# The row maximum of the global attention: one VectorE instruction over four PSUM banks in place of four and a fifth over their results

## What is computed

```python
qh = _split_heads(jnp.einsum('bnq,qi->bni', x, Wq))        # 8 heads x 4096 tokens x 128
kh = _split_heads(jnp.einsum('bmc,ci->bmi', context, Wk))  # 8 heads x 1920 contexts x 128
vh = _split_heads(jnp.einsum('bmc,ci->bmi', context, Wv))
sim = jnp.einsum('hid,hjd->hij', qh, kh) * SCALE
mean = jnp.mean(sim, axis=-1, keepdims=True)
sim = (sim - mean) * ATTN_MATRIX_SCALE + mean
attn = jax.nn.softmax(sim, axis=-1)
out = jnp.einsum('hij,hjd->hid', attn, vh)
```

## Time and profile before

| | us |
|---|---|
| median of 3 runs | 4903.08 (4897.85 to 4910.84) |
| the profiled execution, its own time | 4901.11 |
| its span, first to last instruction | 4899.0 |
| TensorE busy | 4206.9 (86%) |
| VectorE busy | 3463.0 (71%) |
| ScalarE busy | 2265.4 (46%) |
| GpSimd busy | 518.2 (11%) |
| mean granted clock of TensorE, as a share of 2.4 GHz | 0.917 |

### The profile page before, as it was taken

The page is one execution under the profiler, slowest core; times in us unless marked ns, Lnnn a source line. Parts: engine busy times, 40 slices in busy tenths (PEclk is TensorE's granted clock), DMA queues, the critical chain, the costliest instruction groups (busy, mean ns, idle before and its releaser), DMA issues. The chain is left out here.

```text
span 4899.0 us, 72375 instructions
## 1 busy us (share of the span) xinstructions
PE 4206.9 (86%) x23248; PEld 3247.5 (66%) x23248; DVE 3463.0 (71%) x8155; ACT 2265.4 (46%) x5353; POOL 518.2 (11%) x953
## 2 busy tenths in 40 slices
PE   8989979996999999999999999998226888788686
PEld 6867767774787777787777777776014555555554
DVE  7976667666677777777777777777647777777445
ACT  3546645553565655555555655554311222222322
POOL 2320010104000000000000000000301112211300
PEclk9989989997999999999999999998557888888699
DMA  3000000000000000000000000000020000000101
GB/s 85 0 35 0 0 1 0 0 0 17 2 2 4 2 4 1 3 4 2 4 2 4 2 4 1 3 1 4 11 58 5 0 0 0 0 0 1 38 0 34
DMA packets 33807, 41.24 MB, mean 8 GB/s; under 512 B 5180, under 2 KB 30019, under 8 KB 33479
## 3 DMA queue, kind: packets, MB, share of 16 engines
q1 hardware_dynamic: 33544, 38.08, 2.7%
HBM read 33.61 MB, written 4.19 MB: 8 GB/s over the span
## 5 line engine op out<-in xcount | busy, mean ns | idle before, releaser
L1683 ACT ACTIVATE global_prob_t_high<-psum 128x512 fp32r<-128x512 f32 x960 | 569.9, 601 | 588.8 <-PE psum L1797 588.8
L1591 DVE TENSOR_TENSOR global_prob_t_low<-psum,global_prob_t_high 128x512 fp32r<-128x512 f32 x960 | 656.9, 690 | 252.4 <-ACT global_prob_t_high L1683 238.2
L1597 DVE TENSOR_REDUCE global_top<-psum 128x1 f32<-128x480 f32 x1024 | 666.3, 657 | 108.8 <-PE psum L1757 103.7
L1704 ACT ACTIVATE global_prob<-psum,global_bias 128x480 f32<-128x480 f32 x1024 | 674.3, 662 | 17.9 <-DVE global_bias L1600 15.1
L1797 PE MATMUL psum<-ident,global_prob 128*128 128x128 f32 x3840 | 568.4, 273 | 39.1 <-DVE global_prob_t_low L1591 38.0
L1797 PEld LDWEIGHTS psum<-ident,global_prob 128*128 128x128 f32 x3840 | 467.5, 141 | 197.8 <-DVE global_prob_t_low L1591 70.6
L1755 PE MATMUL psum<-global_prob_t_high,global_v_low 128*128 128x512 f32 x960 | 456.1, 475 | 1.0
L1755 PE MATMUL psum<-global_k_high,global_q_low 128*128 128x480 f32 x1024 | 390.7, 382 | 15.1 <-ACT global_prob L1704 12.7
L1757 PE MATMUL psum<-global_k_high,global_q_high 128*128 128x480 f32 x1024 | 392.0, 383 | 0.0
L1756 PE MATMUL psum<-global_k_low,global_q_high 128*128 128x480 f32 x1024 | 388.7, 380 | 0.0
L1756 PE MATMUL psum<-global_prob_t_low,global_v_high 128*128 128x512 f32 x960 | 379.6, 395 | 0.0
(11 more groups left out here) (445 smaller groups left out, 8091.4 us busy)
## 6 DMA issues: line engine op xcount, KB each, us to landing
x_res<-in_x SPq DMA_DIRECT2D x8, 512.0 KB, 9.7
moe_we<-in_expert_t SPq DMA_DIRECT2D x8, 512.0 KB, 7.7
out<-x_res SPq DMA_DIRECT2D x4, 1024.0 KB, 8.4
cho_wqkv<-in_L_ffn_Wqkv SPq DMA_DIRECT2D x2, 1536.0 KB
self_ctx_t<-in_ctx_t SPq DMA_DIRECT2D x2, 1440.0 KB, 12.9
sel_w<-in_L_xattn_W SPq DMA_DIRECT2D x2, 1024.0 KB, 11.9
global_ctx_t<-in_ctx_t SPq DMA_DIRECT2D x1, 1440.0 KB
sel_ctx_t<-in_ctx_t SPq DMA_DIRECT2D x1, 1440.0 KB
```

The costliest lines, as they stand in the source:

```text
L1591: dve.tensor_tensor(dst, psum, high.bitcast(F32), ALU.subtract).then_inc(ready.sem, 1)
L1597: ins = dve.tensor_reduce(top[:, c:c + 1], w.psum[:, c, 0:chunk], AX.X, ALU.max)
L1683: act.activation(dst, psum, ACT.Copy).then_inc(ready.sem, 1)
L1704: act.activation(prob[:, par, j, c * chunk:(c + 1) * chunk], w.psum[:, c, 0:chunk], ACT.Exp, bias=bias[:, j % 2:j % 2 + 1], scale=scale, a ...
```

## The change

`maximum` waits once, for the last of the four chunks, and takes the maximum over the two free dimensions of all four banks in one instruction, straight into `bias`. The tile `top` goes. The multiplication by -scale stays.

```diff
-    top = sb("top", [P, chunks])
...
             def maximum(n, j):

-                for c in range(chunks):
-                    dve.wait_ge(scores_psum.sem, scores_psum.count((n * QT + j) * chunks + c))
-                    ins = dve.tensor_reduce(top[:, c:c + 1], w.psum[:, c, 0:chunk], AX.X, ALU.max)
-                chain.link(ins)
-                chain.link(dve.tensor_reduce(bias[:, j % 2:j % 2 + 1], top[:, :], AX.X, ALU.max))
+                dve.wait_ge(scores_psum.sem, scores_psum.count((n * QT + j) * chunks + chunks - 1))
+                chain.link(dve.tensor_reduce(bias[:, j % 2:j % 2 + 1], w.psum[:, 0:chunks, 0:chunk], AX.XY, ALU.max))
                 dve.tensor_scalar(bias[:, j % 2:j % 2 + 1], bias[:, j % 2:j % 2 + 1], -scale, None,
                                   ALU.mult).then_inc(bias_ready.sem, 1)
```

## The result

The changed kernel takes **5135.93 us** (median of 4 runs, 5132.42 to 5145.42), the kernel before 4905.91 us beside it (4 runs, 4897.85 to 4910.84). The ratio is 1.0474, with an interval of 1.0452 to 1.0495: 4.7% slower. The forecast was 5172 us, 36 us too much; 5135.93 lies inside the range from 5095 to 5215.

A forecast was written before the change was run, and what follows sets the result against it. TensorE was taken as the bound of the changed stage. The profiled 4901 us plus 208 us of delays, mostly waits for low parts, plus 63 us of slow clock gave 5172 us, with a range from 5095 to 5215 us.

The forecast's parts named there:

- What bounds the kernel: In the changed stage TensorE is busy 2119.63 of 2175.00 us, so a saving on VectorE is worth nothing by itself.
- The price of the reduction: One reduction over four banks takes 2.16 us; the multiplication begins 2.24 us behind the last product, 1.32 us later than before.
- Who pays: TensorE waits for late low parts: 1.32 us in tiles 0 and 3, 1.0 in tile 1, 0.04 in tile 2.
- The change of heads: In the 7 quads that change heads, 1.3 us at tile 0, values hide most of the rest: 7 x 1.5 = 10 us.
- some 0.2 us at the end: At the end of a quad that changes heads, the part not hidden by the values, where the exponentials are waited for.
- Ahead of the loop: The first maximum loses 1.3 us, the next three gain 0.4 us each: nothing in sum.
- The clock: Behind 7 in 10 of tile 0's 1.9 us idle stretches, 56 in all, the clock falls, losing 1.6 us each: 63 us.
- Rival 1: The clock holds throughout, leaving only the delays: 4901 + 208 = 5109 us, span 5095 to 5125; chance 0.25.
- the case with the falls: The main forecast, delays plus a falling clock: 5172 us, span 5140 to 5215; chance 0.60.
- Rival 2: VectorE catches up late low parts in its pauses, so only tile 0 pays: 84 us, 4985 us; chance 0.06.
- Rival 3: Faster: where VectorE reaches the maximum after the last product, one instruction beats five; 97 us less, 4804 us; chance 0.03.
- Rivals 4 and 5: 4: slow clock lasts longer or also follows tile 3, above 5215 us, chance 0.04; 5: unseen cover, no difference, chance 0.02.

The follow-up runs named there:

- e1: The kernel before, with its four reductions and the small one, but all waiting for the last product: 5250.36 us, ratio 1.0707.
- e8: The kernel before with the one merged reduction in row tile 0 alone, four reductions in the other tiles: 5002.96 us, ratio 1.0193.
- e12: The kernel before with the one merged reduction in row tile 3 alone, four reductions in the other tiles: 4981.62 us, ratio 1.0148.
- e3: The kernel before with the one merged reduction in row tile 2 alone, four reductions in the other tiles: 4904.57 us, ratio 1.0001.
- e10: The changed kernel with TensorE's loop over the heads written out, so that it has no jump back: 5120.97 us, ratio 1.0425 to the kernel before.
- e6: The changed kernel with `sums` moved on VectorE from behind tile 0's maximum to behind the low part of k = 3: 5084.18 us, ratio 1.0362 to the kernel before.
- e2: The kernel before with an unneeded reduction on VectorE behind each multiplication by -scale, delaying the low parts but not ScalarE: 5075.05 us, ratio 1.0349.
- e7: The changed kernel with four unneeded products on TensorE behind tile 0's `output`, filling part of its wait: 5120.97 us, ratio 1.0435 to the kernel before.
- e9: e5 with TensorE's loop over the heads written out, the other engines keeping their loops: 4879.1 us, ratio 0.9939 to the kernel before.
- e11: e5 with the loops over the heads written out on TensorE, VectorE and ScalarE: 4866.56 us, ratio 0.9915 to the kernel before.
- e5: The kernel before with `sums` moved on VectorE from behind tile 0's maximum to behind the low part of k = 3: 4875.37 us, ratio 0.9939.

## Why the prediction was right, and where its sizes were off

**What bounds the kernel: right.** TensorE was the bound, and 173 us less of VectorE's work were worth nothing. The sign and the mechanism are shown by e1, in which the late start alone, without the new instruction, costs more than the change.

**The price of the reduction: right.** 2.16 us taken, 2158 ns measured; 2.24 us behind the last product, 2.23 measured.

**Who pays: right, tile by tile.** A plain interval was to grow by 3.68 us and grew by 3.46. Tile 0 was put at 1.32 us (1.3 in e8), tile 3 at 1.32 (1.2 in e12), tile 1 at 1.0 (0.9 to 1.0), tile 2 at 0.04 (nothing in e3). The error of 0.2 us is mostly tile 3, and makes 9 us over 40 intervals. The waits for low parts were to rise to about 240 us and rose to 211.2.

**The change of heads: too low.** The step was "some 0.2 us at the end" with "7 x 1.5 = 10 us". By intervals (tiles 1 to 3 of that quad and tile 0 of the next, 0.2 + 1.3 + 1.32 = 2.8 us) that forecast is 20 us for the seven; measured are 34, of which some 26 are delay and 8 falls. I had let the values hide the late low part of k = 14. They do hide TensorE's wait for it, but the start of the next head is not hidden: it follows that low part by about 4 us, with five gaps longer by 1.0 to 1.6 us, and behind four of them the clock fell. e10 shows it: without TensorE's jump the five gaps are gone, and the kernel is 15 us faster.

**Ahead of the loop: too low.** The forecast was "nothing in sum"; measured are 3.0 us up to the first `sums`, of which 1.3 are tile 0 of the first quad, forecast elsewhere, and 1.7 are left. The first maximum lost the 1.3 us. The second and the fourth gained 0.39 us each, but at the third VectorE was not late, as the forecast had it: it waited 1.45 us for the last chunk (reduction at 1249.43), and nothing was gained there.

All delays together were forecast at 208 us and measured at 210.

**The clock: the step that failed.** It was "I take it that the clock falls behind 7 in 10 of these stretches". The idle stretch came out as forecast, 1.87 us for 1.9, and each fall cost what was forecast, 1.58 us for 1.6. But only 11 of some 53 stretches in tile 0 were followed by one. That is 18 us in place of 63, and with the falls at the changes of heads 25. Against the profiled run, 5132.42 us, the forecast was 40 us too high: 38 us of it are the clock and 4 us the shorter rest of the run, less 2 us by which the delays were too low. One case ahead of the loop (1.97 us, followed by a fall) had been taken as the rule for 56 others. The traces of all these kernels together say what that one row could not:

| idle stretch of tile 0 in the loop | kernels | stretches | followed by 1.2 GHz |
|---|---|---|---|
| 1.3 to 1.4 us | e6 | 53 | 0 |
| 1.64 us, 1.74 us | e2 | 54 | 0 |
| 1.71 us (first and last head) | change | 12 | 0 |
| 1.87 us | change | 40 | 11 |
| 1.87 us | e8 | 42 | 13 |
| 1.87 us | e10 | 36 | 10 |
| 2.1 to 2.3 us | e1 | 51 | 20 |

In this place of the loop no fall came behind a stretch of up to 1.74 us, some came behind 1.87 us, and even 2.3 us are no rule. Elsewhere the length says less still. Ahead of the loop of the change a stretch of 1.61 us, which ended at 1244.99, was followed by the 1.2 GHz level (window, busy, granted clock, DMA share, GB/s):

```profile
1245.40:1248.70 3.30, 3.30 (x10) 0.50 0.00 0
```

The very first tile 0 of the loop, in which TensorE has no output to make, stood for 2.24 us in e8 and a fall followed, and for 2.67 us in the change and none did. What decides between two equal stretches of 1.87 us, as those that ended at 2613.26 and 2687.46, was not found.

**The rivals.** Rival 1, that the clock holds, had 5109 us, 27 under the result; the case with the falls had 5172, 36 over it. The truth lies between the two, since the clock holds in 4 of 5 stretches. It is in neither of the two spans of which the range was made, 5140 to 5215 with a falling clock and 5095 to 5125 with one that holds; that the range as a whole contains it owes something to luck. The rule of the Trainium skill's page "TensorE: Matmul & The Clock Gate", section "Why this matters for your kernels" (no idle gaps above about 3 us), which that rival named, is too mild here, since 34 of 118 stretches of 1.87 us were followed by a fall; yet as a forecast of the time it did better than my 7 in 10. Rival 2, the delay that is caught up: refuted by e12, where tile 3 alone costs 74 us. Rival 3, the one instruction wins where VectorE is late at the maximum: true of the second and the fourth maximum ahead of the loop, and of no other. There the multiplication begins 1243.90 - 1241.72 = 2.18 us behind the start of the reduction, where before it was 2.57 us; ahead of the other 254 reductions VectorE waited for the scores, 616.1 us in all. The section on the TRN2 errata of the Trainium skill's page "VectorE: DVE Perf Modes" (larger tiles, a fixed latency paid once) gives its reason for sources in SBUF, and the reduction here reads PSUM; that fewer and larger instructions save a fixed part agrees with the engine's time here, 173 us less, and says nothing of the path. Rivals 4 and 5: neither happened.

## What to carry to other kernels

Between a producer and a consumer that work side by side, piece by piece, a merged instruction saves its overhead and pays its whole length behind the last piece; look at what is queued behind it on its engine and ask how late that may be before the bound engine stands still. The same view read the other way round shows what to gain: what stood between the last score and the first low part (`sums`, 0.45 us of TensorE's wait) could be moved behind the urgent work for 31 us. A row tile in which something else is waited for anyway, as tile 2, takes the merge for nothing, and also gives nothing.

## What the runs showed of the hardware that I had not expected

- **The clock is not decided by the length of an idle stretch alone.** Equal stretches of 1.87 us, in the same place of the same loop, were followed by the 1.2 GHz level in 11 of 40 cases. The slow stretch behind them begins 0.8 to 1.4 us after TensorE has resumed, lasts 3.4 us and costs 1.6; at changes of heads it can begin up to 1.3 us before TensorE resumes (e1), and one of those in the change and three in e12 lasted 6.8 us.
- **Products that nobody needs can pay.** Four of them, 0.9 us long in a wait of 1.87, took away every fall behind tile 0, and 15 us (e7).
- **A jump back in a loop costs time, and the costs of two engines hide one another.** Writing out TensorE's loop alone gave nothing in e9, since VectorE was late behind its own jump. With all three written out, e11 took 4866.56 us against 4875.37 of e5: 8.8 us for five jumps, 1.8 us each. ScalarE's share was not tried by itself.
